# Weights of heads 8 to 15 in another place among the transfers; last latents, first exponent and last rope parts of each batch in another order

## The reference

```python
# x: (2, 1024, 256); 16 heads; query rank 192, key/value rank 64; rope part 64, plain part 128, value 128
c_kv = x @ w_dkv                     # latent of keys and values
c_q = x @ w_dq
k = concat(rope(x @ w_kr), c_kv @ w_uk)      # one rope part for all heads
q = concat(rope(c_q @ w_qr), c_q @ w_uq)
v = c_kv @ w_uv
attn = softmax(q @ k.T / sqrt(192)) @ v      # over 1024 keys, no mask
x = layernorm(x + attn.reshape(b, s, 16 * 128) @ w_o)
# ternary weights: s = mean(abs(w)); q = clip(round(w / s), -1, 1) * s
g = silu(x @ w1q.T) * (x @ w3q.T)            # hidden 682
x = layernorm(x + g @ w2q.T)
```

## Time and profile before

| | |
|---|---|
| median of 3 runs | 905.95 us (899.76 to 906.23) |
| the profiled execution | 906.63 us |
| its span, first to last instruction | 904.8 us |
| busy in the span | PE 867.4, DVE 675.0, ACT 679.5, POOL 614.3 us |
| mean granted clock of PE | 0.983 |

### The profile page before, as it was taken

One profiled execution on the slowest core, in us unless ns is written; L12 is line 12 of the kernel. 1 busy time (PEld: TensorE's weight loads), 2 busy tenths in 40 slices (PEclk: granted clock), 3 DMA queues, 4 the chain that ended last, 5 costly groups with the idle time before them and its releaser, 6 DMA issues.

```text
span 904.8 us, 17011 instructions
## 1 busy us (share of the span) xinstructions
PE 867.4 (96%) x5186; PEld 504.5 (56%) x5186; DVE 675.0 (75%) x1063; ACT 679.5 (75%) x1095; POOL 614.3 (68%) x436
## 2 busy tenths in 40 slices
PE   8989969999999999999999978999999999999996
PEld 6557634544454444548886844444544444446875
DVE  2378987888888888873467988788888887885366
ACT  2454589999999999991352478999999999996142
POOL 0026877887888788883352886788887888887134
PEclk9599999999999999999999999999999999999999
DMA  9753799999999989996501499999989989999201
GB/s 263 197 244 59 170 207 194 165 191 174 172 180 175 175 165 190 174 172 184 180 2 55 108 189 203 178 173 195 173 162 194 169 169 185 174 171 171 99 1 46
DMA packets 424587, 145.81 MB, mean 161 GB/s; under 512 B 408268, under 2 KB 417184, under 8 KB 423776
## 3 DMA queue, kind: packets, MB, share of 16 engines
q1 hardware_dynamic: 423936, 143.43, 78.1%
q0 software_dynamic: 448, 1.57, 0.5%
q10 hardware_dynamic: 160, 0.26, 0.1%
HBM read 23.85 MB, written 7.60 MB: 35 GB/s over the span
## 4 chain that ended last, share of the span: by engine, by line
PE 68%; SPq 9%; DVE 6%; DMA 5%; issue 4%; POOL 4%; ACT 3%; DVEq 0%; ACTq 0%; POOLq 0%
PE Tb L1257 17%; PE OO L1228 12%; PE Sa L1228 11%; PE Sb L1228 7%; PE Ta L1239 5%; SPq L368 4%; SPq L337 3%; PE Sa L1375 3%; PE Sb L1375 2%; DMA PT_dma<-P_parts 2%; POOL turned L447 1%; PE Sb L1267 1%; DMA wuv<-in_L_attn_w_uv_dram 1%; PE OO L1405 1%; ACT probs L627 1%
## 5 line engine op out<-in xcount | busy, mean ns | idle before, releaser
L473 POOL TENSOR_TENSOR P_parts<-probs,P_parts 128x768 f16<-128x768 f32 x256 | 419.9, 1658 | 105.8 <-ACT P_parts L533 105.7
L533 ACT ACTIVATE P_parts<-probs 128x768 f16<-128x768 f32 x256 | 205.6, 842 | 5.1 <-DMA PT_dma<-P_parts 4.0
L920 DVE TENSOR_TENSOR PT_lo<-Ta,PT_hi 128x512 f16<-128x512 f32 x128 | 88.5, 691 | 62.2 <-ACT PT_hi L533 59.7
L896 DVE TENSOR_REDUCE small<-OO 128x1 f32<-128x1024 f32 x96 | 117.1, 1220 | 21.6 <-PE OO L1228 21.6
L1257 PE MATMUL Tb<-PT_dma,V_hi 128*64 128x512 f16 x768 | 131.9, 385 | 0.0
L627 ACT ACTIVATE probs<-OO,small,scales 128x1024 f32<-128x1024 f32 x96 | 115.5, 1204 | 18.7 <-DVE small L899 17.0
L1228 PE MATMUL OO<-K_hi,Q_parts 128*128 128x512 f16 x384 | 115.4, 382 | 11.1 <-ACT probs L627 9.1
L896 DVE TENSOR_REDUCE small<-Sa 128x1 f32<-128x1024 f32 x96 | 116.8, 1217 | 8.5 <-PE Sa L1228 8.5
L627 ACT ACTIVATE probs<-Sa,small,scales 128x1024 f32<-128x1024 f32 x96 | 115.6, 1204 | 4.8 <-DVE small L899 2.5
L1228 PE MATMUL Sa<-K_hi,Q_parts 128*128 128x512 f16 x384 | 115.1, 381 | 3.5 <-ACT probs L627 3.4
L896 DVE TENSOR_REDUCE small<-Sb 128x1 f32<-128x1024 f32 x64 | 77.9, 1217 | 12.1 <-PE Sb L1228 12.1
(11 more groups left out here) (302 smaller groups left out, 1560.9 us busy)
## 6 DMA issues: line engine op xcount, KB each, us to landing
Q_parts<-turned_parts SPq DMA_DIRECT2D x64, 128.0 KB, 2.4
TT<-ternary SPq DMA_DIRECT2D x2, 2304.0 KB, 8.8
Q_parts<-Q_parts SPq DMA_DIRECT2D x16, 256.0 KB, 3.3
PT_dma<-P_parts SPq DMA_TRANSPOSE x256, 3.9
ternary<-tern SPq DMA_DIRECT2D x1, 2304.0 KB, 7.9
xq<-in_L_attn_x_dram SPq DMA_DIRECT2D x2, 1024.0 KB, 10.4
wq_low<-Wq_lo SPq DMA_DIRECT2D x1, 2048.0 KB, 12.2
Wvo_lo<-wvo_low SPq DMA_DIRECT2D x8, 256.0 KB, 4.0
```

What stands on the lines that cost most here:

```text
L473: nc.gpsimd.tensor_tensor(P_parts[:, n % DEEP, 1, :], probs[n % DEEP][:, KP * P:S], P_parts[:, n % DEEP, 0, :], ALU.subtract).then_inc(par ...
L533: return nc.scalar.activation(o, i, ACT.Copy, scale=scale)
L896: nc.vector.tensor_reduce(nmax[:, n % 4:n % 4 + 1], scores_bank(n)[:, :], AX.X, ALU.max, negate=True).then_inc(row_max, 1)
L920: nc.vector.tensor_tensor(PT_lo[place].rearrange("p k (t q) -> p t k q", t=2), T_BANK[:, :].rearrange("p (t k q) -> p t k q", t=2, k=KP), ...
```

## The change

Transfers: part 3 of the heads' weights is issued before w1 and w3, part 4 before w2. Ternary: the sum of w3 is taken behind head 10 and that of w2 behind the last head (into a buffer of its own, `magnitudes`); PE adds the first two after head 12 and the third on its own after head 15; w1 and w3 are made ternary in steps 6 and 7 of DVE's loop, w2 behind it; ACT's high parts of w_qr move behind the sum of w2; PE's transposes of ternary weights wait for the last scales.

Queries: in the last group tile 2 goes to OO and tile 3 to T (the other way round before). Exponent 0 and its copy stand between the two latent copies of ACT; maximum 1 between the latent low parts of DVE; scores 1 before the last query tile. The last group's `turned` and parts have buffers of their own (`turned_end`, `parts_end`, over Wq_lo), so POOL's two additions wait for the last query tile (`q_ps`). DVE makes their parts in steps 0, 2, 4 and 6, and SP moves them ahead of tiles 11 to 14, two transfers each, with the last two latent moves ahead of tiles 9 and 10.

```diff
-            for part in range(3):
+            for part in range(4):
                 absorbed_weights(part, PARTS[part])
                 output_weights(part, PARTS[part])
             sp.wait_ge(pad_ready, 3)
...
-            absorbed_weights(3, PARTS[3])
-            output_weights(3, PARTS[3])
-            sp.dma_start(w2n[:, :, 0:HID], w2.rearrange("(t p) h -> p t h", p=P)).then_inc(w2_in, 16)
             absorbed_weights(4, PARTS[4])
             output_weights(4, PARTS[4])
+            sp.dma_start(w2n[:, :, 0:HID], w2.rearrange("(t p) h -> p t h", p=P)).then_inc(w2_in, 16)
...
+                        if first and n == 8:
+                            for j in range(2):
+                                sp.wait_ge(turned_out[j], (b + 1) * 64 * GROUPS - 64)
+                        if first and n in (9, 10):
+                            t = 4 * (GROUPS - 1) + 2 * (n - 9)
+                            sp.wait_ge(lat_lo, (b + 1) * 4 * GROUPS)
+                            sp.dma_start(Q_parts[64:128, t, :, :], Q_parts[0:64, t + 1, :, :]).then_inc(lat_moved, 16)
-                        if first and n in (3, 5):
+                        if first and n in (11, 12, 13, 14):
+                            j = n // 13
                             sp.wait_ge(lat_moved, (b + 1) * 32 * GROUPS)
-                            rotary_moves(GROUPS - 1, n // 2 - 1)
...
+                            sp.wait_ge(rope_lo[j], (b + 1) * GROUPS)
+                            for s in range((n + 1) % 2 * 2, (n + 1) % 2 * 2 + 2):
+                                sp.dma_start(Q_parts[32 * j:32 * j + 32, 4 * (GROUPS - 1) + s, :, :],
+                                             parts_end[32 * s:32 * s + 32, j, :, :]).then_inc(turned_out[j], 16)
...
+                        if g == GROUPS - 1:
+                            pool.wait_ge(q_ps, (b + 1) * 4 * GROUPS)
-                        if g >= 1:
+                        elif g >= 1:
                             pool.wait_ge(rope_lo[j], b * GROUPS + g)
...
-                if h in (8, 9):
-                    absolute_sum(h - 7)
-                if h >= 12:
-                    rotary_high((h - 12) // 2, h % 2)
+                if h == 10:
+                    absolute_sum(1)
+            absolute_sum(2)
+            for c in range(4):
+                rotary_high(c // 2, c % 2)
...
                     latents_high(g, 0)
-                    latents_high(g, 1)
                     if g == GROUPS - 1:
                         act_.wait_ge(ff_out, 16)
                         exponent(b * PAIRS * TILES, 0)
+                        part_high(b * PAIRS * TILES, 0, None)
+                    latents_high(g, 1)
...
-                if 5 <= j < 8:
-                    ternary_below(j - 5)
+                if j >= 6:
+                    ternary_below(j - 6)
...
+            last_scales()
+            ternary_below(2)
+            ternary_weight(2)
...
-                        if first and n in (0, 2):
-                            rotary_parts_high(GROUPS - 1, n // 2)
+                        if first and n in (0, 4):
+                            rotary_parts_high(GROUPS - 1, n // 4)
                         transposed_low(pair * (TILES // 2) + n // 2, n + 1)
-                        if first and n in (0, 2):
-                            rotary_parts_low(GROUPS - 1, n // 2)
+                        if first and n in (2, 6):
+                            last_parts_low(n // 4)
...
+            pe.wait_ge(abs_done, 2)
+            pe.wait_ge(ff_scale, 2)
+            mm(Sb[:, 2:3], ones[:, :], asum[:, 2:3], start=True, stop=True).then_inc(ff_mean, 1)
             for n in range(9):
+                if n == 0:
+                    pe.wait_ge(ff_scale, 5)
                 turn_ternary(n)
...
                             scores(b * PAIRS * TILES, 0, 0, b * PAIRS * 2)
+                            pe.wait_ge(rope_mul, b * 4 * GROUPS + 4 * GROUPS)
+                            scores(b * PAIRS * TILES + 1, 1, 0, b * PAIRS * 2)
                         query_terms(g, j, range(5))
...
-                        if first and n == TILES - 2:
+                        if not (first or last) and n == TILES - 2:
                             pe.wait_ge(lat_moved, b * 32 * GROUPS + 32 * GROUPS)
```

90 lines of the change are left out of this document (50 added, 40 removed).

## The result

The changed kernel is slower by 0.7%: its median is 909.63 us over 20 executions (904.66 to 914.64), that of the kernel before 902.95 us over 20 executions made beside them (897.33 to 906.76). The ratio is 1.0072, with a 95% interval of 1.0052 to 1.0092. The forecast was 898.5 us with a range up to 904.0. The profiled execution took 912.33 us around a span of 910.5 (before: 906.63 and 904.8).

What follows compares the result with a forecast made beforehand. TensorE was taken as the bound in steady pairs, except in the weights and each batch's first pair. Weights -5.4 us and transition -1.0 in each of two batches, from the 905.95 median, gave 898.5 us (893.5 to 904.0).

Steps and rivals of the forecast that it cites:

- The weights, as a difference of two profiles: Weights stage: x turned near 49.3 us instead of 54.66, a gain of 5.4 us (3 to 7.4).
- Head 8's stall: Weights stage: TensorE's 3.21 us wait for head 8's w_uv transfer goes, since those weights land by 16.3 us.
- VectorE as the end of the stage: Weights stage: VectorE's last ternary weight ends it at 46.7 us, 6.1 us before 52.8.
- the two excesses: VectorE's extra 0.94 and 0.38 us beside GpSimd on w2n; twice their sum, 2.6 us, allowed (0 to 3.9).
- The base of the sum: Starting time: the profiled 906.63 us was taken as an ordinary execution, the median of three being 905.95.
- The clock before head 12: Weights stage: TensorE waits 1.4 us (0.8 to 2.1) for head 12's weights and the clock stays full.
- Rival A: Clock falls in the wait before head 12; stage ends at 52.2 us, total 901.5 us; chance 0.12.
- The start of the pair: First pair of a batch: exponent 2 0.6 us later, exponent 7 at 125.0 instead of 126.29; 1.0 us gained a batch.
- slack 2.6: First pair, SyncE's queue: transposes 2.7 us late at pair's end, rope-part buffers have 2.6 us to spare; cost put at nothing.
- its bad case: SyncE 5.2 us late at 2.0 us a transpose; ScalarE waits up to 2.6 us at tiles 12 to 17.
- The first prefetch: SyncE's new wait ahead of it is for moves landed by then: nothing, at most 0.1 us a pair.
- Rival C: Transition gives nothing, eaten by GpSimd's late start and SyncE's moves: 900.6 us, 901.6 or 903.8 with losses; chance 0.18.

Runs made afterwards that it cites:

- w_only: Kernel before with only the weights part: changed order of transfers, ternary order and scales; 902.64 us, ratio 0.9998.
- w_exp: Changed kernel with last rope parts and moves handled as in the kernel before, keeping weights part, banks and early exponent; 904.28 us, ratio 1.0010.
- moves_pf: Changed kernel with latent moves ahead of tiles 6 and 8, rope moves spread over pair 1, prefetches ahead of pairs 2, 4, 6, 7; 902.72 us, ratio 0.9999.
- lat_early: Changed kernel with only the two last latent moves put back where the kernel before has them; 905.28 us, ratio 1.0020.
- t_only: Kernel before with only the transition part (banks, first exponent, last rope parts and their moves); 914.46 us, ratio 1.0121.

## Why the prediction was wrong

**The weights, as a difference of two profiles: right.** Head 8's stall gone, a short wait before head 12, the clock at full to 36 us, VectorE as the end of the stage: all there. -5.4 us was forecast, -6.6 measured. Two sizes in it were off and nearly cancel: the products ended at about 34.7, not 36.1, and the collisions with GpSimd cost more than the two excesses doubled. The last of the scales took 0.99 us for a column instead of some 0.15, `below` 2.13 and the weight 2.74, against 1.01 and 1.80, and the weight before them 2.47: 3.6 us over, where 2.6 were allowed. That the sum came out so well is in part luck: head 12 started at 26.74, ahead of the 27.5 to 28.8 that were given for its transfers; in the other profiles with the new order and no filler it started between 26.29 and 28.34.

**The base of the sum: wrong.** The step that failed is "The profiled execution took 906.63 ...; the median of three is 905.95, so it is an ordinary one". It was one of the upper group, and the worst of four profiles at this place: x turned at 54.66, against 52.49, 50.16 and 44.94. Their mean is 50.6; that of the seven profiles with the new weights order and no filler is 49.5 (47.99 to 51.53). The weights part is worth about 1 us, not 5.4, by these means, and w_only against the kernel before (0.9970 to 1.0025) can't tell it from nothing. It gains where the old order falls to half clock, and loses 3 us or more where it doesn't (44.94, one profile, against 47.99 at best), since VectorE's chain is longer. Three times of the kernel before, 899.76 beside 906.23 and 905.95, had shown the spread, and I took no note of it.

**The clock before head 12: wrong as a rule.** "This is shorter than the 2.23 us after which the clock had not fallen, so I let it stay at full". The changed kernel's own profile had it at full, after a wait of 0.18 us. But with the new order the clock fell near there in three of its eight profiles (at 28.7 to 29.6 us, after waits of 0.54, 0.74 and 1.15 us: w_exp, moves_pf, lat_early), and stayed up in w_only after 1.36 us. Rival A, which had 0.12, is thus a share of the executions, not another outcome. Where the clock fell so, x was turned at 49.84 to 51.53, a little better than the rival's 52.2.

**The start of the pair: right.** Exponent 2 was 0.8 us late (forecast 0.6), exponent 7 ahead by 1.6 (forecast 1.3), both low parts took 1.22 us.

**SyncE: the step that made the kernel slower.** The step that failed is "slack 2.6, so I put it at nothing", with a lateness of 2.7 us. The lateness measured is 5.9 us at tile 14, 6.1 in batch 1; the prediction had 5.2 as its bad case. And ScalarE did not wait once, up to 2.6 us at tiles 12 to 17, but again and again: 0.4, 1.3, 2.1 and 2.5 us at tiles 14, 16, 18 and 20. By the columns of the table the transition gave 1.8 + 0.9 us at the first exponents, and took 8.0 + 6.3 in the three pairs behind them (means of the four profiles before: 53.3, 114.1, 158.5, 113.3), 11.6 us in all where -2.0 was forecast.

Five terms were mis-sized or missing. The ten moves took 7.6 us of the queue, not 6.9. Transposes between the latent moves took up to 2.39 us, not 1.65. Rope moves wait for the last latent move to land, 3.7 to 4.9 us after its issue; that wait (tile 10's transpose ends at 132.75, the first rope move goes out at 133.58) was not in the sum. The first prefetch comes on top while SyncE is still late, and it was held to be free since its wait is "for moves landed by then". And the time that ScalarE waits makes TensorE idle, after which the clock fell in this execution and cost another 3 to 4 us in pair 1. Rival C named the place and the sign, and its dearest form, 1.6 us a batch, was too small by a factor of three to four.

The 11.6 us are again those of one execution, and a slow one. The medians moved by +6.7 us (902.95 to 909.63) where -7.4 were forecast. With about -1 for the weights some 8 us are left for the transition (an estimate from the medians and the means above), so of the 14.1 us between forecast and result about 4 are the weights' and 10 the transition's. Taking its causes out one at a time took the ratio of 1.0072 to 1.0051 (prefetch alone; 1.0023 to 1.0080, so this step alone is not clear of noise), 1.0020 (latent moves alone), 1.0026 (moves alone, with two prefetches together) and 0.9999 (moves and prefetch), with w_only at 0.9998. That the queue of SyncE is where the loss arises is shown by these four; how much of it goes with the clock is read from two profiles.

## What to carry to other kernels

Where a stage of a kernel can run at either clock, profile the kernel before several times before pricing a change of that stage: the change may only make permanent what half of the executions do already. When moves are put into a queue that catches up by tenths of a microsecond a tile, add up each move, the landing that the next one waits for and the next block of transfers behind them; a lateness equal to the slack is a stall, and not "nothing", and it is paid at every tile until the queue has caught up. Where TensorE idles briefly for a transfer, 14 idle transposes ahead of the wait took away the executions at the low clock with three lines of code; that they make this kernel faster is not shown (0.9951 to 1.0013).

## What the runs showed of the hardware

The length of a wait does not tell whether the clock falls. In the weights it fell to half after waits of TensorE for a head's transfers of 0.54, 0.69, 0.74, 1.15, 1.49, 2.10, 3.21 and 3.22 us, and not after 0.18, 0.35, 0.73 and 1.36 us. Once down there it stayed at half for 10 to 27 us, with TensorE busy for 74 to 100% of that time (for all of 24.1 to 48.0 us in the profile before, and for all of the 27.3 us in t_only).

The same transfer of w_uv for heads 8 to 11 made head 8 wait 0, 0.69, 2.10 and 3.21 us in four executions of one program.

A VectorE operation on a single column took 0.99 us beside GpSimd's Wq_lo and 0.15 us without it. The Trainium skill (SBUF - State Buffer, "SBUF: two separate sides") has these two engines take a shared port pair for a whole instruction when VectorE reads two inputs in SBUF, and by that rule even the smallest one waits. The rows agree: the operation ended at 41.31, just behind the end of GpSimd's second operation on Wq_lo at 41.29, and the scales made just before from Sb, one input each, took 0.14 us.
